# Lower halves of the first weights and the conditioning's halves on GpSimd instead of VectorE, while VectorE makes one-hot rows

## The reference, cut to what matters

```
h = relu(layernorm(x))
cond = silu(emb @ f_w1 + f_b1) @ f_w2 + f_b2          # emb: sin and cos of noise * 32 frequencies; cond: 1250 x 16
for i in range(4):
    y = xn(h) * (1 + cond @ s1_w[i] + s1_b[i]) + cond @ b1_w[i] + b1_b[i]
    q, k, v = y @ wq[i] + bq[i], y @ wk[i] + bk[i], y @ wv[i] + bv[i]
    h += softmax over the edges(q[src] . k[dst]) v[dst] @ wo[i] + bo[i]
    h += relu(cond_norm(h) @ m_w1[i] + m_b1[i]) @ m_w2[i] + m_b2[i]
x = x + h
x = x + gcn(relu(gcn(relu(layernorm(x)), W1, b1)), W2, b2)
```

## Time and profile before

| | before |
|---|---|
| median of 3 runs | 1967.62 us |
| the profiled execution | 1967.23 us, its span 1965.5 us |
| TensorE busy (over the span) | 1890.2 us, 96% |
| VectorE busy | 1373.7 us, 70% |
| ScalarE busy | 783.1 us, 40% |
| GpSimd busy | 449.4 us, 23% |
| the stretch 15 to 182 us: PE / DVE / POOL busy | 148.6 / 144.9 / 4.0 us |

### The profile page before, as it was taken

How to read it: one execution, slowest core, us unless ns; L and a number is a source line. 1 busy time by engine, 2 the same in 40 slices (tenths; PEclk the granted TensorE clock), 3 DMA queues, 4 the chain that set the end, 5 groups by cost and what they waited for, 6 DMA issues and landing times. The chain is left out here.

```text
span 1965.5 us, 33581 instructions
## 1 busy us (share of the span) xinstructions
PE 1890.2 (96%) x11664; PEld 1562.3 (79%) x11664; DVE 1373.7 (70%) x2830; ACT 783.1 (40%) x1528; POOL 449.4 (23%) x525
## 2 busy tenths in 40 slices
PE   6988999999999999999999999999999999899999
PEld 3545888999889899988898999889989998775443
DVE  7887658888875588888657888885498888730111
ACT  1332455555432355544224555542255554330000
POOL 1000243112342422213325111252241113500000
PEclk9999999999999999999999999999999999999999
DMA  4112553111300112112102110301121106110001
GB/s 136 47 43 44 154 160 105 37 37 29 117 33 22 58 39 63 34 39 83 40 25 66 54 36 25 121 1 43 48 58 37 36 26 177 42 37 0 0 21 31
DMA packets 50719, 108.36 MB, mean 55 GB/s; under 512 B 18143, under 2 KB 18195, under 8 KB 50608
## 3 DMA queue, kind: packets, MB, share of 16 engines
q1 hardware_dynamic: 50608, 106.87, 18.5%
HBM read 83.60 MB, written 23.25 MB: 54 GB/s over the span
## 5 line engine op out<-in xcount | busy, mean ns | idle before, releaser
L785 ACT ACTIVATE PT<-ps 125x500 fp32r<-125x500 f32 (+1 forms) x480 | 214.2, 520 | 324.3 <-PE ps L1596 324.3
L1503 PE MATMUL ps<-PT,V 125*128 125x250 f32 x2400 | 313.2, 284 | 1.6 <-DVE PT L1173 1.6
L1503 PE MATMUL ps<-kT,qg 128*125 128x512 f32 (+1 forms) x1440 | 302.5, 354 | 6.8 <-DVE nmx L1157 5.5
L1503 PEld LDWEIGHTS ps<-PT,V 125*128 125x128 f32 x2400 | 289.6, 190 | 2.9 <-DVE PT L1173 2.9
L1503 PEld LDWEIGHTS ps<-kT,qg 128*125 128x125 f32 x1440 | 246.0, 186 | 57.3 <-issue 9.6
L1173 DVE TENSOR_TENSOR PT<-ps,PT 125x500 fp32r<-125x500 f32 (+1 forms) x480 | 253.0, 582 | 2.1 <-ACT PT L785 1.8
L1157 DVE CUSTOM_DVE_ANT_0 SB<-ps,bt 125x1250 f32<-125x1250 f32 x140 | 203.9, 1457 | 47.0 <-PE ps L1503 44.6
L1596 PE MATMUL ps<-ident,pbuf 125*125 125x125 f32 x1600 | 202.4, 274 | 13.6 <-DVE pbuf L1166 13.6
L1596 PEld LDWEIGHTS ps<-ident,pbuf 125*125 125x125 f32 x1600 | 187.3, 189 | 16.6 <-DVE pbuf L1166 15.9
L779 ACT ACTIVATE pbuf<-SB,nmx 125x1250 f32<-125x1250 f32 x140 | 188.1, 1344 | 8.7 <-DVE nmx L1157 7.4
L1166 DVE TENSOR_SCALAR pbuf<-pbuf,rden 125x1250 f32<-125x1250 f32 x160 | 149.8, 936 | 5.6
(11 more groups left out here) (194 smaller groups left out, 2715.4 us busy)
## 6 DMA issues: line engine op xcount, KB each, us to landing
bt<-edge_bias_scratch SPq DMA_DIRECT2D x40, 546.9 KB
q_scratch<-qc SPq DMA_DIRECT2D x16, 500.0 KB, 2.6
qc<-q_scratch SPq DMA_DIRECT2D x16, 500.0 KB, 4.8
counts_scratch<-cblk SPq DMA_DIRECT2D x10, 546.9 KB
c_rows<-counts_scratch SPq DMA_DIRECT2D x10, 546.9 KB
edge_bias_scratch<-b_rows SPq DMA_DIRECT2D x10, 546.9 KB
counts<-counts_scratch SPq DMA_DIRECT2D x10, 546.9 KB
wm<-in_L_gnn_wo_dram SPq DMA_DIRECT2D x4, 1024.0 KB, 8.4
```

What stands on the lines that cost most here:

```text
L785: sc.activation(PT[:, h % 2, 0, a:b, u * T:(u + 1) * T], ps_T[0:T, i, 0:(b - a) * T].rearrange("p (t n) -> p t n", n=T), ACT.Copy).then_in ...
L1503: e = mm(out_, lhs(a), rhs(b), start=start and i == 0, stop=stop and i == 2)
```

## The change

The three lower halves of the weights and the three instructions on `condS` go from VectorE's stream to GpSimd's, ahead of and behind `split_ln(0)`. On GpSimd the weights wait for ScalarE's upper halves and for the third matmul of the embedding (`emb_h`), because `wa` lies over `embT`.

```diff
@@ gpsimd @@
-            pool.wait_ge(s["condS"], 1)
+            def split_wa_low(i):
+
+                pool.wait_ge(s["wa_hi"], 3 - i)
+                pool.wait_ge(s["emb_h"], 3)
+                g.tensor_tensor(wa[:, i, 1], wm[:, i], wa[:, i, 0].bitcast(F32), ALU.subtract).then_inc(s["wa"], 1)
+
+            def cond_split():
+
+                pool.wait_ge(s["condT"], 3)
+                g.tensor_copy(condS[0:C + 1, :], condT[:, :])
+                g.tensor_copy(condS[32:32 + C + 1, :], condT[:, :]).then_inc(s["condS0"], 1)
+                pool.wait_ge(s["condS0"], 1)
+                g.tensor_tensor(condS[64:64 + C + 1, :], condT[:, :], condS[0:C + 1, :].bitcast(F32), ALU.subtract).then_inc(s["condS"], 1)
+                pool.wait_ge(s["condS"], 1)
+
+            for i in (2, 1, 0):
+                split_wa_low(i)
             split_ln(0)
+            cond_split()
             cond_chunk(0, PROJECTED[0])
@@ vector @@
-            def split_wa_lo(i):
-
-                dve.wait_ge(s["wa_hi"], 3 - i)
-                v.tensor_tensor(wa[:, i, 1], wm[:, i], wa[:, i, 0].bitcast(F32), ALU.subtract).then_inc(s["wa"], 1)
-            def cond_split():
-
-                dve.wait_ge(s["consts"], CONSTS)
-                dve.wait_ge(s["condT"], 3)
-                v.tensor_copy(condS[0:C + 1, :], condT[:, :])
-                v.tensor_copy(condS[32:32 + C + 1, :], condT[:, :]).then_inc(s["condS0"], 1)
-
-            def cond_low():
-
-                dve.wait_ge(s["condS0"], 1)
-                v.tensor_tensor(condS[64:64 + C + 1, :], condT[:, :], condS[0:C + 1, :].bitcast(F32), ALU.subtract).then_inc(s["condS"], 1)
@@ for t in range(NT) of vector @@
                 if t == 9:
-                    cond_low()
                     front_norm(0, PROJECTED[0])
                 one_hots(t)
...
                 if t == 3:
                     node_aggregate()
-                if 4 <= t <= 6:
-                    split_wa_lo(6 - t)
                 if t == 5:
                     node_rstd()
-                if t == 7:
-                    cond_split()
```

## The result

The changed kernel takes 1979.26 us (median of 4 runs, 1977.93 to 1979.96), the kernel before 1967.78 in the same comparison (4 runs, 1966.53 to 1968.07). The ratio is 1.0059, 95% interval 1.0041 to 1.0076: slower by 11.5 us, where 13.1 were forecast. The profiled execution has a span of 1977.3 us against 1965.5.

What follows compares the result with a forecast made beforehand. VectorE's one-hot rows were taken to bound the counting inside every tile, TensorE just following. Costs of 17.7 and 6.1 us less gains of 10.7 gave +13.1 us, 1980.7 us, range 1971 to 1987.

Steps and rivals of the forecast that it cites:

- Every microsecond of VectorE inside a tile is on the path: Counting: VectorE bounds each tile at 0.62 us a chunk; between tiles only what exceeds TensorE's 3.8 us counts.
- GpSimd and VectorE take turns by whole instructions, the 16-bit rows too: One-hot rows in the counting: charged the whole of GpSimd's time, 17.7 us for weights and 6.1 for conditioning.
- Rivals 1 and 2: 1: 16-bit rows run unhindered, 1957 us, chance 0.09; 2: GpSimd starts only where VectorE is idle, 1966, chance 0.08.
- 4.5 us for a subtraction of 128 x 2048: GpSimd's weight subtractions in tile 4: 4.5 us each for 2048 elements a partition, upper bound 5.2.
- The narrow 125 x 125 rows run beside: Tile 4: small one-hot rows of 0.16 us taken as free; one source row passes between GpSimd instructions, -0.8 us.
- The clock: Behind blocks at tiles 4 and 7 TensorE falls to 1.2 GHz, +1.5 each; tiles 8 and 9 regain -1.8 and -1.5.
- the forecast 17.7: Tile 4, weights and split_ln(0) on GpSimd: 16.2 us of blocked one-hot rows plus 1.5 of slow clock.
- Tile 7, +6.1: Conditioning on GpSimd at tile 7's start: 4.6 us of blocked rows plus 1.5 of slow clock.
- Ahead of tile 9, -4.4: VectorE's subtraction leaves and split_ln no longer falls on the norm: 4.0 us instead of 8.3.
- the 1.4 us ahead of tile 6: Behind tile 5, VectorE comes 2.28 us earlier without its subtraction and TensorE's 1.40 us wait goes: -1.4.

Runs made afterwards that it cites:

- e4_reordered: Kernel before, all its VectorE work kept there in another order, GpSimd's split_ln moved behind tile 3: 1956.9 us, ratio 0.9943 to before.
- e5_gated: Changed kernel, same GpSimd instructions, each started by a VectorE semaphore at a tile border: 1963.9 us, ratio 0.9977 to the kernel before.
- e2: Changed kernel with the weights left on VectorE, only the conditioning on GpSimd: 1967.6 us, ratio 0.9997 to the kernel before.
- e3: Changed kernel with each 128 x 2048 subtraction cut into four of 128 x 512: 1980.6 us, ratio 1.0063 to the kernel before.
- e1: Kernel before with only the three lower halves of the weights moved to GpSimd: 1979.6 us, ratio 1.0060 to before.

## Why the prediction was right, step by step

- *Every microsecond of VectorE inside a tile is on the path.* Right: the difference on TensorE moves with the blocks and with the borders only.
- *GpSimd and VectorE take turns by whole instructions, the 16-bit rows too.* Right, and now shown for that pair: 4.84 us in place of 0.54. Rivals 1 and 2 are out: GpSimd's subtractions follow each other at once, and are not stretched to tile borders. The Trainium skill's rule ("SBUF — State Buffer", Who interferes with whom) agrees with these rows, also in what it lets pass: an instruction with one SBUF input outside the 2-port modes is free of it, as the statistics in e4_reordered were.
- *4.5 us for a subtraction of 128 x 2048.* Right. Three took 13.64 us together, and one that met no source row took 4.51 (e5_gated, at 107.63 us).
- *The narrow 125 x 125 rows run beside.* Wrong: they take their turn as well (4.49 us at 85.24). So beside the three subtractions not one source row a hand-over passed but one in two. It made little difference in time: the fourth chunk came 15.7 us late (98.63 against 80.86 + 3 x 0.62 + 0.22) where 16.2 were forecast.
- *The clock.* Mostly right. After the blocks the granted clock was at half, the 1.2 GHz level:

```profile
100.00:104.00 4.00, 4.00 (x13) 2.46 (x12) 2.92 (x8) 0.00 (x0) 0.00 (x0) 0.50 0.00 0
...
152.00:156.00 4.00, 3.45 (x11) 2.18 (x12) 3.35 (x11) 0.98 (x2) 0.56 (x1) 0.57 0.00 0
164.00:168.00 4.00, 3.00 (x15) 1.66 (x15) 3.29 (x12) 1.35 (x5) 0.00 (x0) 1.00 0.48 125
```

  Tile 4's remaining 15 chunks took 11.76 us, where before they took 11.52 - 3 x 0.62 = 9.66: 2.1, not 1.5. So the +17.8 of tile 4 meets the forecast 17.7 in part by luck: the block was 0.5 shorter and the slow clock cost 0.6 more. Tiles 8 and 9 started at the full clock, as forecast.
- *Tile 7, +6.1.* Measured +5.3: the cost was taken 0.8 too high.
- *Ahead of tile 9, -4.4.* Measured -5.4. The term was mis-sized in the loads: I kept 3.16 us between `rstd` and the first row, and it was 180.81 - 178.29 - 0.16 = 2.4. The bare loads took 1.31 us there in place of 2.04. In every run where GpSimd did not fall on the norm (e2, e3, e5 too) they took 1.31 to 1.33, and 2.05 in e1, where it did. Why is not shown:

```profile
178.29 0.16 DVE L1101 TENSOR_TENSOR rstd<-nt_c,r 125x2 f32<-125x2 f32 x1
178.49 1.00 DVE L1087 TENSOR_SCALAR pbuf<-z,mv,rstd 125x512 f32<-125x512 f32 x2
180.81 0.26 DVE L1005 TENSOR_SCALAR oh_dst<-iota,edgeT 125x125 bf16<-125x125 f16 x1 [1.31 <-issue]
```

These last two are 0.8 and 1.0 us; with the small differences of the table they are the 1.6 us by which the sum was too high. What e1 and e2 add: the loss is all in the weights, and moving them gained only the 1.4 us ahead of tile 6. Behind tiles 4 and 6 VectorE's 2.28 us were free before.

## What to carry to other kernels

Before work goes to an idle GpSimd, ask what VectorE runs at that moment: beside operations that it excludes, as the one-hot rows here, nearly each of GpSimd's microseconds is one of VectorE's (17.5 us of GpSimd in tile 4 cost VectorE 15.9), and a GpSimd subtraction takes twice VectorE's time (4.5 against 2.28 us). Look first for places where VectorE's work costs nothing: here a long instruction right ahead of register loads covers their 2.1 us, and the reordering gained 11 us where the move lost 11.5. The same kernel moved `split_ln` beside the statistics as well, so the 11 us are not the order on VectorE alone. If GpSimd must do it, start it by a semaphore at a border, beside statistics or loads, not when its inputs happen to be ready: that took 15 us off here (e5_gated).

## What was not expected of the hardware

- TensorE's clock in tiles 0 and 1 differs from execution to execution of code that is the same up to there: tile 1 took 13.49 us in the profile before, 12.47 in e1_weights, 11.23 in e4_reordered. So single profiles differ by some 2 to 4 us for no reason of the kernel (e3_pieces: the profiled execution took 1976.4 us, the median is 1980.6), and a difference of that size needs the timed rounds.
- The clock fell in e5_gated behind a wait of TensorE of only 0.27 us (tile 5: 12.50 against 11.15 us), where in the kernel before waits of 0.78 and 1.40 us had cost nothing. In e4_reordered a wait of 0.79 us did cost 1.3 us, in the tile that took 11.52 before:

```profile
78.23 12.78 PE L1447 MATMUL ps<-oh_src,oh_dst 125*125 125x512 bf16 x54 [0.79 <-DVE oh_src L991]
```

  Two pairs of profiles differ here in one thing more. Where the granted clock in 13 to 45 us had been 0.89 (before and e2_cond), tile 4 kept the full clock behind waits of 0.78 and 0.77 us; where it had been 1.00 (e4_reordered and e5_gated), it fell in tile 4 behind 0.79 (0.57 in 79 to 83 us in both). I can't say from these runs what decides it.
